# Quantised heads: exponents and lowering to 8 bits on GpSimd; attention's last batch on VectorE

## What is computed

```python
qkv8 = requant(qkv)                       # scale, round, clip to -128..127
a = einsum('bhnd,bhmd->bhnm', q, k)
a = a - max(a);  a = a + floor(a/2) - floor(a/16);  a = maximum(a, 15*x0)
q_ = floor(a / x0);  r = a - x0*q_
e = floor((r/2 - x0) * 2**(15 - q_))
factor = floor(2**31 / sum(e))
sm = floor(e * factor / 2**24);  ctx = einsum('bhnm,bhmd->bhnd', sm, v)
```

```python
dots = einsum('bhid,bhjd->bhij', q, k) * scale;  se = dots.mean(heads)
dots = where(diagonal, -inf, dots);  keep = top_k(dots, 96)
attn = softmax(where(keep, dots, -inf) + se);  out = attn @ v @ w_out + b_out
```

## Time and profile before

| what | us |
|---|---|
| median of 3 runs (3259.19 to 3260.62) | 3259.4 |
| the profiled execution | 3258.02 |
| its span, first to last instruction | 3256.2 |
| quantised heads, from the clearing to the end of the last context | 1696.6 to 1989.4 |
| attention's end, from the last search to the last row added | 2999.5 to 3030.2 |

### The profile page before, as it was taken

How to read it: one execution, slowest core, us unless ns; L and a number is a source line. 1 busy time by engine, 2 the same in 40 slices (tenths; PEclk the granted TensorE clock), 3 DMA queues, 4 the chain that set the end, 5 groups by cost and what they waited for, 6 DMA issues and landing times. The chain is left out here.

```text
span 3256.2 us, 39009 instructions
## 1 busy us (share of the span) xinstructions
PE 2358.5 (72%) x12582; PEld 1428.7 (44%) x12622; DVE 2285.9 (70%) x5872; ACT 1592.5 (49%) x2954; POOL 1047.8 (32%) x578
## 2 busy tenths in 40 slices
PE   5879985789888876899821112878889787774467
PEld 4646662334334334599621111422222466664345
DVE  5743344898989996211379998788888699998531
ACT  3232114666665642111127773777778546654211
POOL 2000003888888983577200000000000033444032
PEclk9979996999999998899955555899999899997578
DMA  2230002222222223311100001334435400000231
GB/s 56 35 122 1 1 21 79 81 102 104 91 91 104 91 90 89 117 40 40 60 0 1 0 1 37 102 129 143 149 119 187 133 1 1 1 1 1 92 119 58
DMA packets 86726, 219.12 MB, mean 67 GB/s; under 512 B 35773, under 2 KB 53403, under 8 KB 76955
## 3 DMA queue, kind: packets, MB, share of 16 engines
q1 hardware_dynamic: 80380, 204.38, 18.6%
q0 software_dynamic: 6144, 12.25, 1.2%
HBM read 199.46 MB, written 25.03 MB: 69 GB/s over the span
## 5 line engine op out<-in xcount | busy, mean ns | idle before, releaser
L2518 DVE TENSOR_TENSOR_SCAN mam_st<-mam_da,mam_st 128x512 f32<-128x512 f32 x384 | 441.1, 1204 | 39.7 <-ACT mam_da L2458 36.0
L2286 POOL TENSOR_TENSOR mam_st<-mam_du,mam_b_rows 128x1536 f32<-128x1536 f32 x128 | 441.6, 3450 | 82.1 <-PE mam_ysum L2356 58.1
L2356 PE MATMUL mam_ysum<-mam_st,held_ident 128*128 128x512 f32 x768 | 363.9, 611 | 0.0
L1905 ACT ACTIVATE codw_hp<-cod_up,cod_b 128x512 f32<-128x512 f32 x512 | 316.8, 704 | 83.5 <-PE cod_up L1765 83.4
L2458 ACT ACTIVATE mam_da<-mam_delta,mamw_decay 128x508 f32<-128x508 f32 x384 | 251.6, 681 | 178.5 <-DVE mam_st L2518 143.4
L2657 POOL TENSOR_TENSOR att_probs<-att_se,att_neg 128x1536 f32<-128x1536 f32 x16 | 55.0, 3440 | 795.9 <-DVE att_neg L2867 795.9
L2356 PEld LDWEIGHTS mam_ysum<-mam_st,held_ident 128*128 128x128 f32 x768 | 150.3, 197 | 153.7 <-issue 150.5
L2867 DVE MATCH_REPLACE8 att_neg<-att_top,att_neg 128x128 f32<-128x128 f32 x768 | 201.2, 276 | 0.0
L702 DVE SCALAR_TENSOR_TENSOR held_h<-x_dn,held_gate,held_h 128x192 f32<-128x192 f32 x256 | 89.1, 411 | 154.5 <-PE x_dn L664 152.8
L2047 DVE TENSOR_TENSOR codw_hp<-codw_hp,cod_gate 128x512 f32<-128x512 f32 x256 | 163.6, 681 | 46.8 <-ACT codw_hp L1905 45.5
L1765 PE MATMUL cod_up<-cod_zr,cod_w1r 96*128 96x512 bf16 x512 | 177.9, 386 | 15.8 <-ACT codw_hp L1905 9.4
(11 more groups left out here) (575 smaller groups left out, 5376.4 us busy)
## 6 DMA issues: line engine op xcount, KB each, us to landing
codw_wide_gates<-gate_scratch SPq DMA_DIRECT2D x128, 512.0 KB, 3.9
mam_b_rows<-b_scratch SPq DMA_DIRECT2D x32, 1024.0 KB, 6.7
mam_c_rows<-b_scratch SPq DMA_DIRECT2D x32, 1024.0 KB, 4.6
slot_scratch<-in_slot_fresh SPq DMA_DIRECT2D x2, 3860.0 KB
sw_w<-in_L_w SPq DMA_DIRECT2D x1, 6144.0 KB, 18.6
grw_w<-in_L_w SPq DMA_DIRECT2D x1, 5376.0 KB, 42.8
grw_w<-in_L_w SPq DMA_DIRECT2D x1, 4608.0 KB
sw_w<-in_L_w SPq DMA_DIRECT2D x1, 4608.0 KB, 33.9
```

The costliest lines, as they stand in the source:

```text
L1905: nc.scalar.activation(hp[step % HOLD][:, j, :], up[u % BANKS][:], ACT.Gelu_apprx_tanh, bias=b1[:, sub * HT + f:sub * HT + f + 1]).then_in ...
L2286: nc.gpsimd.tensor_tensor(st[it % N_ST][:], du[r % 2][:], along(b_rows[:, p % RING, n % PIECE, :], 1, [P, MC, MT]), ALU.mult)\
L2356: last = nc.tensor.matmul(ysum[:, c, :], m.ident[:], st[it % N_ST][:, c, :], start=False, stop=(it % DS == DS - 1))
L2518: nc.vector.tensor_tensor_scan(fs, fa, fs, 0.0, ALU.mult, ALU.add).then_inc(scanned, 1)
```

## The change

In the quantised heads the lowering (`to_8_bits`) and the exponents leave VectorE's list and become GpSimd's: `to_8_bits(0)`, `to_8_bits(1)`, then for each batch `powers(b)` and `to_8_bits(b + 2)`. `powers` waits for the rounding (semaphore `rounded`); VectorE's product of power and rest waits for `powered`. In attention GpSimd makes the logits of 15 batches only. For the last one VectorE makes them itself, in two passes with a minimum where GpSimd adds a bar, then the maxima; and it scales the last batch in one product where ScalarE had twelve.

```diff
 # attention_stage, GpSimd
-            for b in range(NB):
+            for b in range(NB - 1):
                 logits(b)
                 bar(b)
                 if b >= 2:
                     add_out(b - 2)
+            add_out(NB - 3)
             add_out(NB - 2)
             add_out(NB - 1)
 # ScalarE
-                if b < NB:
+                if b + 1 < NB:
                     normalise(b)
 # VectorE
+            def last_logits():
+                b = NB - 1
+                x, cut = probs[b % 2][:], neg[b % NRING][:]
+                v.wait_ge(searched, b + 1)
+                v.wait_ge(pt_ready, b - 1)
+                c.step(nc.vector.tensor_tensor(x, along(se[b % NRING][:], 1, heads), cut, ALU.subtract))
+                c.step(nc.vector.scalar_tensor_tensor(x, cut, BAR, x, ALU.add, ALU.min))
+                nc.vector.tensor_reduce(down[b % 2][:], x, AX.X, ALU.max, negate=True).then_inc(lifted, 1)
+
+            def last_normalise():
+                b = NB - 1
+                x = probs[b % 2][:]
+                v.wait_ge(parted, b + 1)
+                nc.vector.tensor_tensor(x, x, along(part[b % 2][:], 2, heads), ALU.mult).then_inc(probs_ready, 1)
...
-            highest(NB - 1)
+            last_logits()
             invert(NB - 1)
+            last_normalise()
 # quant_heads_stage, GpSimd
+            c = Chain(pool, fetched)
+
+            def to_8_bits(b):
...
+            def powers(b):
+                pool.wait_ge(rounded, b + 1)
+                if b:
+                    pool.wait_ge(floored, b)
+                nc.gpsimd.tensor_scalar(flat(power), flat(quot), -float(1 << 23), float((127 + 15) << 23),
+                                        ALU.mult, ALU.add).then_inc(powered, 1)
+
             nc.gpsimd.memset(qk8[:], 0.0).then_inc(cleared, 1)
+            pool.wait_ge(cleared, 1)
+            for b in range(2):
+                to_8_bits(b)
+            for b in range(NB):
+                powers(b)
+                if b + 2 < NB:
+                    to_8_bits(b + 2)
 # VectorE, rest(b)
-                c.step(nc.vector.tensor_scalar(flat(quot), flat(quot), RND, -RND, ALU.add, ALU.add))
+                nc.vector.tensor_scalar(flat(quot), flat(quot), RND, -RND, ALU.add, ALU.add).then_inc(rounded, 1)
+                v.wait_ge(rounded, b + 1)
                 nc.vector.scalar_tensor_tensor(fx, flat(quot), z.neg_x0[:, 0:1], fx, ALU.mult, ALU.add)\
                     .then_inc(rest_ready, 1)
-                c.step(nc.vector.tensor_scalar(flat(power), flat(quot), -float(1 << 23), float((127 + 15) << 23),
-                                               ALU.mult, ALU.add))
 # floors(b)
                 v.wait_ge(halved, b + 1)
+                v.wait_ge(powered, b + 1)
```

More of the change, by code:

```diff
@@ L3055, in quant_heads_stage @@
         ctx_ps = s.psum("ctx_ps", [P, 512])
[L3056 removed]
+        names = ("cleared fetched rounded powered taken qkt_ready qkt_copied sc_ready max_ready x_ready grids_ready clipped scaled_ready "
                  "rest_ready halved floored sm_ready smt_ready smt_copied ctx_ready ctx_kept dve").split()
[L3058 removed]
+        (cleared, fetched, rounded, powered, taken, qkt_ready, qkt_copied, sc_ready, max_ready, x_ready, grids_ready, clipped, scaled_ready,
          rest_ready, halved, floored, sm_ready, smt_ready, smt_copied, ctx_ready, ctx_kept, dve) = (
@@ L3071, in _ @@
         def _(pool):
-            nc.gpsimd.memset(qk8[:], 0.0).then_inc(cleared, 1)
+            c = Chain(pool, fetched)
+            def to_8_bits(b):
+                c.step(nc.gpsimd.tensor_tensor(scaled[:], z.qkv[:, b, :], z.requant_row[:], ALU.mult))
+                c.step(nc.gpsimd.tensor_scalar(scaled[:], scaled[:], RND, RND + QMAX, ALU.add, ALU.min))
+                if b:
+                    pool.wait_ge(qkt_ready, b)
+                if b >= 4:
+                    pool.wait_ge(ctx_ready, b - 3)
+                for n in range(2):
+                    nc.gpsimd.tensor_scalar(
+                        qk8[:, n, :, :, 0:HD0],
+                        scaled[:, n * D:(n + 1) * D].rearrange("p (g j d) -> p g j d", g=HG, j=HJ),
+                        RND - QMAX - 1.0, -RND, ALU.max, ALU.add)
+                nc.gpsimd.tensor_scalar(v8[b % 4][:], scaled[:, 2 * D:3 * D], RND - QMAX - 1.0, -RND, ALU.max, ALU.add)\
+                    .then_inc(taken, 1)
+                pool.wait_ge(taken, b + 1)
+            def powers(b):
+                pool.wait_ge(rounded, b + 1)
+                if b:
+                    pool.wait_ge(floored, b)
+                nc.gpsimd.tensor_scalar(flat(power), flat(quot), -float(1 << 23), float((127 + 15) << 23),
+                                        ALU.mult, ALU.add).then_inc(powered, 1)
+            nc.gpsimd.memset(qk8[:], 0.0).then_inc(cleared, 1)
+            pool.wait_ge(cleared, 1)
[5 more added lines that the diff above has]
+                    to_8_bits(b + 2)
         @block.tensor
@@ L3191, in _ @@
             c = Chain(v, dve)
-            def to_8_bits(b):
-                c.step(nc.vector.tensor_tensor(scaled[:], z.qkv[:, b, :], z.requant_row[:], ALU.mult))
-                c.step(nc.vector.tensor_scalar(scaled[:], scaled[:], RND, RND + QMAX, ALU.add, ALU.min))
-                if b:
-                    v.wait_ge(qkt_ready, b)
-                if b >= 4:
-                    v.wait_ge(ctx_ready, b - 3)
-                for n in range(2):
-                    nc.vector.tensor_scalar(
-                        qk8[:, n, :, :, 0:HD0],
-                        scaled[:, n * D:(n + 1) * D].rearrange("p (g j d) -> p g j d", g=HG, j=HJ),
-                        RND - QMAX - 1.0, -RND, ALU.max, ALU.add)
-                nc.vector.tensor_scalar(v8[b % 4][:], scaled[:, 2 * D:3 * D], RND - QMAX - 1.0, -RND, ALU.max, ALU.add)\
-                    .then_inc(taken, 1)
-                v.wait_ge(taken, b + 1)
             def maxima(b):
@@ L3246, in floors @@
                 v.wait_ge(floored, b + 1)
-            v.wait_ge(cleared, 1)
             c.step(nc.vector.memset(rnd[:], RND))
             c.step(nc.vector.tensor_tensor(shift[:], z.half[:], z.inv_x0[:], ALU.mult))
-            for b in range(2):
-                to_8_bits(b)
             maxima(0)
@@ L3258, in _ @@
                 rest(b)
-                if b + 2 < NB:
-                    to_8_bits(b + 2)
                 floors(b)
```

2 lines of the change are left out of this document (removed).

## The result

The changed kernel takes 3279.3 us (median of 4 runs, 3275.76 to 3281.83) against 3259.3 before: 1.0063 times, 95% interval 1.0050 to 1.0076, slower by 20 us. The profiled execution has a span of 3277.7 us. Forecast was 3260.1 with a range to 3272; the result lies outside.

A forecast was written before the change was run, and what follows sets the result against it. VectorE was taken to bound the quantised heads, and a chain without a second batch the end of attention. Start +6.8, next stage +1.9, batches -2.8 and attention -5.15 summed to +0.75 us on 3259.4: 3260.1 us, range 3252 to 3272.

The forecast's parts named there:

- What bounds the kernel, and the exclusion: Heads' stage goes at VectorE's pace; VectorE and GpSimd exclude each other for whole instructions, so 0.2 us gained a batch, -2.8 us.
- T0: Heads, each batch: the end of the rounding step L3225, from which the prediction counts times inside a batch.
- The third rival: Heads' batches: GpSimd's one-input steps don't exclude VectorE, so -12.0 us in place of -2.8, time 3250.9; chance 0.10.
- I take the same for GpSimd's one-input steps: Heads' batches: assumed they exclude VectorE for a whole instruction, as two-input products do, though no row shows a meeting.
- Price of GpSimd's lowering: Heads: product 1.45 us, one-input steps 0.65 for 576 numbers and 0.35 for 192; with the program switch, start +6.8 us.
- I take 0.65 and 0.35: Heads' lowering on GpSimd: us for one-input steps of 576 and 192 numbers, near the row of 1467 ns for 1536.
- My upper bound: Heads' lowering: one-input steps at the two-input product's price, 1.45 and 0.59 us; the stage's start then costs 8.3 us.
- They end near T0+8.0: Heads' batches: remaining lowering steps, 1.7 us, lie beside VectorE's sum and end before TensorE's transposes at T0+8.37, so nothing waits.
- The change of program: GpSimd's switch between reductions and element work: 5.7 us at the heads' start, and +1.9 us at the next stage's reduction.
- The rival that it is cheap or hidden: Heads' start and next stage: without either cost of switching GpSimd's program, 5.7 + 1.9 us less, 3252.5; chance 0.10.
- GpSimd first at the ports: Rival in the heads: GpSimd's exponents precede VectorE's rest step at T0, +7.9 us in place of -2.8, time 3270.8; chance 0.16.
- End of attention: Last batch of attention: exponentials 3.3 us earlier, one VectorE product for ScalarE's twelve -1.85, together -5.15 us.

The follow-up runs named there:

- step_prices: Changed kernel plus fourteen one-input GpSimd steps at the start of the heads' stage: multiply-add 1.46 us for 1536 numbers, add-minimum 5.4; no kernel time given.
- fast_pairs: Changed kernel with GpSimd's lowering rewritten in multiply-add and minimum-maximum steps, one instruction more: 3262.8 us.
- like_pairs: Changed kernel with GpSimd's lowering regrouped into add-add, then maximum-minimum, as many instructions as before: 3280.1 us.
- all_four: Changed kernel with multiply-add/minimum-maximum lowering begun behind VectorE's product, query and key written together, early GpSimd program changes, ScalarE's weights ahead of the copy: 3259.4 us.
- exponents_only: Changed kernel with the lowering back on VectorE, so of the heads' work only the exponents are GpSimd's: 3265.1 us.
- attention_only: Kernel before with only the changed attention stage, heads as before: 3256.5 us, and 3251.5 when measured again.

## Why the prediction was wrong

**What bounds the kernel, and the exclusion.** Right for the steps that the sum rests on. Exponents to T0+3.17 (measured 3.18), GpSimd's product to T0+4.62 (4.57), the product of power and rest to T0+6.24 (6.19). The third rival, that one-input steps don't exclude, fell: the exponents took 3.04 us beside the rest step and 1.47 in the one batch in which they came first. The Trainium skill's rule ("SBUF — State Buffer", Who interferes with whom), an exclusive lock, agrees with 3.04 against 1.47. "I take the same for GpSimd's one-input steps" went too far all the same: the lowering's dear steps of 192 numbers held neither VectorE's short steps nor its product L3278, whose two inputs in SBUF should have waited by that rule (1.76 us, as in before), and the measurement decides.

**Price of GpSimd's lowering.** This is the step that failed. "I take 0.65 and 0.35, near the one-input row, since these steps have one input": the measured prices are 2.15 and 0.87. The rows of before that I went by were minimum-maximum and add-multiply; the lowering's steps are add-minimum and maximum-add, and step_prices shows 3.5 ns a number for those against 0.95 (1.46 us for 1536). My upper bound, the two-input product's price, was no bound: 1.45 and 0.59. The lowering took 6.4 us at the start instead of 3.35, +3.1. "They end near T0+8.0" became T0+12.07, and the cover on which I costed them at nothing, the transposes at T0+8.37, was gone by 3.7 us. Of these 4.1 us some 3 are the prices (4.76 us against 1.7) and 1.1 is L3103 behind L3278, since the steps now reached past the sum and the short steps into a product. I had written that up to 0.4 us a batch would come back if it were short; it was 0.96 (18.01 against 17.05 in fast_pairs), 0.63 of it by ScalarE's list and most of the rest by the scores. The batches brought +10.7 instead of -2.8. With prices as I had taken them, fast_pairs, they brought -2.5.

**The change of program.** Right as a mechanism, in both places, and the second switch at +2.2 (forecast +1.9). The first was mis-sized: I took 5.73, a change to reductions, for one to element work, which takes 6.8 to 7.6 here. With the lowering's price: +11.1 at the start instead of +6.8. The rival that it is cheap or hidden fell.

**GpSimd first at the ports.** It came true once. In batches 0 to 14 GpSimd's exponents start 0.14 to 0.16 us behind T0 and VectorE's rest step 0.04; in batch 15 GpSimd starts 0.08 behind, and took the ports first:

```profile
1996.95 3.12 DVE L3260 SCALAR_TENSOR_TENSOR qh_x<-qh_quot,quant_neg_x,qh_x 128x1536 f32<-128x1536 f32 x1
```

That is +1.3, which I had priced (3.1 us for the step) but put into a rival for all batches. In like_pairs, fast_pairs and all_four, with the same starts, VectorE came first in batch 15: a lead of 0.04 us does not decide, one of 0.10 always did. exponents_only has the same 0.04 in fifteen batches: VectorE came first in fourteen and GpSimd in the last.

**End of attention.** Forecast -5.15. The exponentials start 8.53 us behind the last search in the runs in which TensorE ran batch 14's mixture at the low clock, as forecast (8.6), and one product replaces the twelve: the scaling ends 1.8 us behind the reciprocal, as forecast (2.2 in the runs in which GpSimd's add took the ports first). The rest is the clock. From the last search to the next stage it took 32.0 and twice 35.3 us without this half, and 25.4 to 29.5 with it. In the changed kernel's profile the exponentials start at 7.23 us, 1.3 earlier, since batch 14's mixture found full clock; from the end of the scaling to the next stage this profile and that of before both take 11.4 us. Two rows show it: the stretch in which the mixture ran (24 products in 1.53 us, granted clock 1.00, the 2.4 GHz level) and, of attention_only, part of the same mixture (0.50, the 1.2 GHz level):

```profile
3032.00:3034.00 2.00, 1.53 (x24) 1.29 (x24) 0.80 (x1) 0.37 (x2) 0.00 (x0) 1.00 0.00 0
```

```profile
3002.00:3004.00 2.00, 1.22 (x12) 1.22 (x14) 1.20 (x1) 0.73 (x1) 0.00 (x0) 0.50 0.00 0
```

GpSimd's add of batch 14's row met VectorE's last product as forecast, 2.21 us instead of 0.59 when VectorE was first, and nothing waited for it.

**Sum.** +11.1, +10.7, +1.3, -0.3, +2.2 and -6.6 make +18.4 of the two profiles; their spans differ by 21.5, of which 1.9 arose ahead of the heads and some 1 between them and attention's end, in stages that are the same in both.

## What to carry to other kernels

A step that moves to another engine is priced by a row with the same operation, not by one with the same shape: here the pair of operations alone made a factor of 3.7, and a two-input row was no upper bound for a one-input step. Where an edit is costed at nothing because something else hides it, size the cover against the worst price and look who is queued behind the one that waits: a late transpose cost little by itself, but the copy behind it held ScalarE's whole list. Work given to GpSimd beside VectorE was free beside VectorE's reductions (here the sum and the maxima), and in other stages of this kernel beside the search (0.28 us a step with and without GpSimd's logits) and the scan (1.20 us with and without GpSimd's products); beside VectorE's two-input steps in SBUF and its short steps, the reciprocal apart (0.23 either way), the two took turns, except where GpSimd's step was a dear one of 192 numbers.

## What the runs showed of the hardware that I had not expected

- On GpSimd multiply-add, add-multiply and minimum-maximum take 1.46 to 1.47 us for 1536 numbers, and add-add, add-minimum, maximum-add and maximum-minimum 5.4; a bf16 output changes nothing (0.86 us for 192 either way, among the dear ones). The order of the pair goes with the price: minimum-maximum 0.67 us for 576, maximum-minimum 2.13 (no run had both with the same constants). The Trainium skill ("GPSIMD Engine Reference", 4.1 Engine selection) has one-input work at about line rate; the first group, 0.95 ns a number where VectorE's rounding of the same 1536 takes 0.62, comes near that, the second, 3.5, does not, and the measurement decides.
- GpSimd's change from reductions to element work took 6.8 to 7.6 us, the one back 5.6 to 6.2; it starts as soon as the queue reaches it, and exponents_only had it at no cost behind a clearing, 18.8 us ahead of the first exponents.
- VectorE's steps of 12 numbers with one input are held by GpSimd's cheap one-input steps (0.17 to 0.49 us), its reductions are not (1.75 us either way). GpSimd's dear steps of 192 numbers held neither these (0.17) nor a two-input product (1.76).
